# Loading the second layernorm's tiles one by one instead of in pairs

## What is computed

```python
def _layernorm(x, axis=-1, eps=1e-5):
    m = jnp.mean(x, axis=axis, keepdims=True)
    v = jnp.var(x, axis=axis, keepdims=True)
    return (x - m) / jnp.sqrt(v + eps)
...
def _L0_ffn_ref(x, w_gate, w_up, w_down):       # weights int32, scaled by 1/127
    gate = jnp.einsum('bsd,hd->bsh', x, wg)
    up = jnp.einsum('bsd,hd->bsh', x, wu)
    h = jax.nn.silu(gate) * up                   # HIDDEN = 3072
    return jnp.einsum('bsh,dh->bsd', h, wd)
...
x = x + _L0_attn_ref(_layernorm(x, axis=-1), ...)
x = x + _L0_ffn_ref(_layernorm(x, axis=-1), w_gate, w_up, w_down)
```

## Time and profile before

| | us |
|---|---|
| median of 2 runs | 1505.18 (1502.39 to 1507.97) |
| the profiled execution | 1504.06 |
| its span on the slowest core (6) | 1502.5 |
| spans of the other cores | 1481.6 to 1500.1 |
| from the first load of the second layernorm to TensorE's first matmul after it | 824.28 to 993.62 |

### The profile page before, as it was taken

The page is one execution under the profiler, slowest core; times in us unless marked ns, Lnnn a source line. Parts: engine busy times, 40 slices in busy tenths (PEclk is TensorE's granted clock), DMA queues, the critical chain, the costliest instruction groups (busy, mean ns, idle before and its releaser), DMA issues.

```text
span 1502.5 us, 17675 instructions; the slowest of 8 cores (1481.6 to 1502.5 us)
## 1 busy us (share of the span) xinstructions
PE 934.5 (62%) x5815; PEld 446.7 (30%) x5892; DVE 513.6 (34%) x928; ACT 330.7 (22%) x691; POOL 136.0 (9%) x193
## 2 busy tenths in 40 slices
PE   0024365666576666666653000059999999999997
PEld 0002232333233223332331000024444444444443
DVE  0022226456645664566474333102112222210110
ACT  0031622532253315331031121011111111100000
POOL 2000000010101010100010000010111111100100
PEclk9967577778877787688766555579999999999999
DMA  9903220221213121311111334963443443303322
GB/s 143 171 1 97 45 54 0 49 58 50 98 30 71 56 98 29 72 56 43 29 51 70 106 84 91 166 89 33 43 43 31 40 43 39 46 30 112 103 93 98
DMA packets 144456, 99.97 MB, mean 67 GB/s; under 512 B 123504, under 2 KB 123504, under 8 KB 144368
## 3 DMA queue, kind: packets, MB, share of 16 engines
q0 software_dynamic: 72816, 81.02, 26.0%
q1 hardware_dynamic: 71552, 17.83, 6.3%
HBM read 93.86 MB, written 16.78 MB: 74 GB/s over the span
## 4 chain that ended last, share of the span: by engine, by line
PE 52%; DVE 20%; DMA 11%; issue 6%; another core or an unknown queue 5%; ACT 4%; DVEq 1%; SPq 1%; POOL 0%; ACTq 0%; POOLq 0%
PE p_d L952 11%; PE p_g L913 11%; PE p_u L926 11%; PE p_fr L339 5%; DVE s_nL L360 3%; DVE s_nL L435 3%; PE p_py L475 3%; DMA s_wd<-wdi 3%; DMA s_x2T<-s_a 3%; DVE s_ht L667 3%; DMA s_x<-x2d 2%; DVE s_y L731 2%; PE p_fr L475 2%; PE p_pp L575 2%
## 5 line engine op out<-in xcount | busy, mean ns | idle before, releaser
L913 PE MATMUL p_g<-s_x2T,s_wgu 128*128 128x512 bf16 x753 | 181.8, 382 | 181.0 <-DMA s_wgu<-wui 180.2
L926 PE MATMUL p_u<-s_x2T,s_wgu 128*128 128x512 bf16 x752 | 180.0, 379 | 0.8
L952 PE MATMUL p_d<-s_wd,s_hff 128*128 128x512 bf16 x753 | 165.1, 379 | 2.0 <-DVE s_hff L932 1.2
L932 DVE SCALAR_TENSOR_TENSOR s_hff<-p_u,s_act 128x512 bf16<-128x512 f32 x96 | 66.4, 692 | 287.1 <-PE p_u L926 262.1
L913 PEld LDWEIGHTS p_g<-s_x2T,s_wgu 128*128 128x128 bf16 x768 | 75.2, 98 | 272.2 <-issue 182.4
L339 PE MATMUL p_fr<-s_xlnT,s_wg 128*128 128x512 bf16 (+1 forms) x312 | 80.9, 422 | 67.0 <-DMA s_xlnT<-s_xln 60.1
L919 ACT ACTIVATE s_act<-p_g 128x512 f32<-128x512 f32 x96 | 57.3, 597 | 270.1 <-PE p_g L913 270.1
L952 PEld LDWEIGHTS p_d<-s_wd,s_hff 128*128 128x128 bf16 x768 | 74.9, 98 | 92.2 <-issue 1.7
L926 PEld LDWEIGHTS p_u<-s_x2T,s_wgu 128*128 128x128 bf16 x768 | 75.1, 98 | 91.0 <-issue 0.5
L575 PE MATMUL p_pp<-s_wo,s_E 128*128 128x512 bf16 x250 | 72.8, 457 | 25.4 <-DVE s_xr L600 23.4
L705 PE MATMUL p_py<-s_V,s_P 64*64 64x64 bf16 x256 | 29.9, 237 | 89.9 <-DVE s_P L641 89.9
(11 more groups left out here) (109 smaller groups left out, 1131.1 us busy)
## 6 DMA issues: line engine op xcount, KB each, us to landing
s_x<-x2d POOLq DMA_DIRECT2D x32, 512.0 KB, 5.0
s_x<-xs POOLq DMA_DIRECT2D x18, 512.0 KB, 7.6
s_xr<-xs POOLq DMA_DIRECT2D x16, 512.0 KB, 3.8
x2d<-s_xr POOLq DMA_DIRECT2D x16, 512.0 KB, 2.9
out<-s_x POOLq DMA_DIRECT2D x16, 512.0 KB, 3.1
s_wd<-wdi POOLq DMA_DIRECT2D x1, 6144.0 KB, 41.6
s_wgu<-wgi POOLq DMA_DIRECT2D x24, 256.0 KB, 4.3
s_wgu<-wui POOLq DMA_DIRECT2D x24, 256.0 KB, 5.3
```

The lines of the kernel that those rows point to most:

```text
L913: addD("t", lambda t, buf=buf, t4=t4, j=j, pb=pb: t.matmul(p_g[pb][:], s_wgu[buf][:, TILE * j:TILE * (j + 1)], s_x2T[:, 2048 * j + 512 * t ...
L926: addD("t", lambda t, buf=buf, t4=t4, j=j, pb=pb: t.matmul(p_u[pb][:], s_wgu[buf][:, 1024 + TILE * j:1024 + TILE * (j + 1)], s_x2T[:, 2048 ...
L932: addD("v", lambda v, hc=hc, t4=t4, pb=pb: v.scalar_tensor_tensor(s_hff[:, 2048 * hc + 512 * t4:2048 * hc + 512 * (t4 + 1)], p_u[pb][:], S ...
L952: addD("t", lambda t, ts=ts, buf=buf, hf=hf, hcc=hcc: t.matmul(p_d[buf][:, 512 * hf:512 * (hf + 1)], s_hff[:, 2048 * hcc + TILE * ts:2048 ...
```

## The change

The grouping of the loads is taken away. Each tile's load is issued on its own, ahead of that tile's other instructions, with the same wait for the a2 of two tiles before; each tile waits for its own load. Since each load closes the count, each load now also waits on GpSimd until the load before it has landed. Number, size and buffers of the loads are the same.

```diff
-        if tt % 2 == 0:
-            for t2 in (tt, tt + 1):
-                dmaD("g", GX, lambda g, t2=t2: g.dma_start(
-                    out=s_x2[:, 1024 * (t2 % 2):1024 * (t2 % 2 + 1)],
-                    in_=x2d.ap()[TILE * t2:TILE * (t2 + 1), :]),
-                    wait=([(VE, a2_done[t2 - 2])] if t2 >= 2 else []))
-            ld_pair = O.close_epoch(GX)
-        ld = ld_pair
+        dmaD("g", GX, lambda g, tt=tt, buf=buf: g.dma_start(
+            out=s_x2[:, 1024 * buf:1024 * (buf + 1)],
+            in_=x2d.ap()[TILE * tt:TILE * (tt + 1), :]),
+            wait=([(VE, a2_done[tt - 2])] if tt >= 2 else []))
+        ld = O.close_epoch(GX)
```

## The result

| | us |
|---|---|
| before, median of 8 runs | 1506.85 |
| changed kernel, median of 9 runs | 1475.86 (eight of them between 1474.1 and 1478.1) |
| ratio | 0.980, interval 0.9786 to 0.9814 |
| the profiled execution, changed kernel | 1475.86 |
| its span on the slowest core (6 again) | 1474.3 |

The gain is 2.0%, just at the bound of what counts as a change here: 1479 was forecast, with 1471 to 1491 as the range.

A forecast was written before the change was run, and what follows sets the result against it. The layernorm was taken as bound by a latency chain with an unhidden load per pair; six gaps shortened by about 4.05 us each plus 1.3 gave 25.6 off 1504.06, 1478.5, by the median 1479 us; range 1471 to 1491.

The forecast's parts named there:

- The bound: Layernorm tiles, 824 to 944 us: a chain of latencies; each pair pays for an unhidden load, 34.3 us of waiting.
- First tile: Start of the layernorm: load 0 no longer waits for load 1, so the first a2 comes 1.3 us sooner.
- The transpose loop: Layernorm tiles: a2, transpose, next a2 is the longest loop and sets the period, 6.54 us for all 13 gaps.
- The cost of a transpose beside a load need not be guessed: Layernorm tiles: today's odd load, issued 0.58 us behind the even tile's transpose, already shows the order all tiles will have.
- Compute loop: Layernorm tiles: with the transpose landed at once, an a2 follows the a2 before by 4.97 us.
- Load loop: Layernorm tiles: loads issued 1.47 us behind an a2 stay hidden, with 2.5 us of cover at the median.
- The tail: Behind tile 13's a2: down weights still take 41.6 us, so the 25.6 us gained pass to the end whole.
- Rival D: Behind tile 13: down weights take longer or GpSimd stands at load 15; half the gain lost, 1492 us; chance 0.05.
- Rival A: Layernorm tiles: transposes slow down under denser loads, gaps up to 7.6 us, time 1493 us; chance 0.11.
- Rival B: Layernorm tiles: load and transpose take turns, every gap 10.6 us, time 1532 us; chance 0.03.
- Rival C: Layernorm tiles: a period as on core 5 on all cores, 5.91 us, gain 33.8, time 1471 us; chance 0.13.

The follow-up runs named there:

- e1: Changed kernel with two buffers for a2, so an a2 waits for the transpose of two tiles before: 1471.6 us, 0.977 of before.
- e5: Changed kernel with three buffers for loaded tiles and the load of tile tt + 2 issued behind the sum of tile tt: 1459.3 us, 0.971 of before.
- e6: Changed kernel with a small 128x64 fill on GpSimd ahead of each load from tile 2 on: 1467.0 us, 0.977 of before.
- e8: Changed kernel with three load buffers, late loads, down weights in 24 parts, first two blocks' gate and up weights loaded inside the layernorm: 1424.7 us, 0.947 of before.
- e2: Changed kernel with each load from tile 2 on issued only after the sum of the tile before it: 1474.4 us, 0.980 of before.
- e4: Changed kernel with a semaphore for each of the two load buffers, so no load waits for the load before it: 1485.0 us, 0.985 of before.

## Why the prediction was right

Core 6, execution against execution. The span fell by 28.2 us: 29.05 in the 13 gaps (109.29 less 80.24) and 1.2 at the first tile, less 0.4 for a later start, 0.4 in the tail and 1.2 behind the first matmul. The forecast was 25.6. The medians moved by 31.3; the 3 us between that and these two executions are not explained.

- **The bound** (a chain of latencies; each pair pays once for a load): right, the wait of the sum went from 34.3 to 1.1 us.
- **First tile**, 1.3 us: 1.2. From the first load's issue to the first a2 8.93 us before, 7.74 after.
- **The transpose loop sets the period**: right in the changed kernel, as e1 shows. Its **size** was the term most off: 6.54 forecast, 80.24 / 13 = 6.17 on core 6, 5.94 over all cores, both under the 6.2 to 7.1 that I had called the forecast. The a2 waited 24.6 us in 11 gaps where I had written 32 in 13. The two gaps at tiles 8 and 9 give 2.5 of the 4.8 us of difference, and that is luck: nothing in my sum made them short. The remaining 11 on core 6 average (80.24 - 4.97 - 5.63) / 11 = 6.33, the other 2.3 us: I had averaged seven gaps of one core, with 7.12 and 7.60 among them. Over all eight cores those gaps of before average 6.14, close to the 6.06 of the changed kernel outside tiles 8 and 9. The eight-core mean was there to be read.
- **"The cost of a transpose beside a load need not be guessed"**: right, and more so than I knew. The offset stayed at 1.47 us in all but a few tiles, and with it the 5.2 us. I took the 5.2 for what a transpose costs beside a load; it is what it costs beside a load issued at that moment. Where the load comes at 1.82 or later it takes 3.0 to 4.0.
- **Compute loop** 4.97: the exact length of twelve gaps in e5. **Load loop**: I gave it 2.5 us of cover; it ran out only at tiles 9 and 10, where the gaps were short (0.8 and 0.3 us of waiting).
- **The tail** (41.6 us of down weights, passed on whole): 42.1 on core 6; from its issue to that of the next weights 42.5 before and 44.0 after, mean of eight cores. Rival D existed with 1.6 us (first matmul 51.4 us behind tile 13 before, 53.0 after), not with half of the gain.
- **Rival A** (denser loads slow the transposes): landings of 4.6 to 5.7, two of 3.0 and 3.2 aside, against 4.8 to 6.5 before; it did not occur. **Rival B** (taking turns): it did not occur. The rule behind both, that all transfers share the 16 DMA engines, is not refuted, but the size of the cost to the transpose is 2.1 us or nearly nothing, by offset.
- **Rival C** (a period like core 5's) is where the measurement leaned: 5.94 over all cores, and on core 6 a gain close to the 30.1 us asked for over 2%. I had given it 0.13; a mean over cores would have given more.

## What to carry to other kernels

Where two engines start a transfer on the same event, look at the distribution of their landing times and not at the median alone: a few short ones among many long ones (3.2 among 5.2 here) can mean that the overlap costs more at one offset than at another, and a start a third of a microsecond later (1.81 for 1.47 in e6) may be nearly free. Then delay one of the two and measure, as e6 and e5 do. A count that stands for two loads makes the first reader wait for the second load; one count for each was worth 4.4 us for each pair here (28.5 us over the 13 gaps, mean of eight cores), most of a load's 5.1. And what follows the repaired chain is the next bound: here one transfer of 42 us that nobody needed for over 300 us, in front of 6 us of weights that everybody waited for.

## What the runs showed of the hardware

- A DMA transpose of a 128x1024 bf16 tile took 4.1 to 6.5 us when the next 512 KB load from GpSimd was issued 1.4 to 1.7 us behind the start of the a2 (all of 462 transposes of tiles 0 to 12, in all kernels here but e8), and 3.0 to 4.0 us when it was issued at 1.82 or later (all of 461). From 1.70 to 1.82 both occur, 61 of 197 over 4 us, and there the cores differ: 51 of 97 took over 4 us on cores 0, 2, 4 and 6, 10 of 100 on cores 1, 3, 5 and 7. Why is open.
- The packets in the trace (the pieces in which the DMA engines move a transfer) say what is slow. A transpose is 1,024 packets of 256 bytes and 32 of 4 bytes. In the changed kernel 87 transposes took over 4 us and 17 less. The last 256-byte packet of the 87 ended 3.5 to 3.6 us behind the start of the a2, just as that of the 17 (3.5 to 3.8). The last 4-byte packet ended at 3.5 to 3.8 in the 17 and at 4.7 to 6.4 in the 87. So the overlap does not slow the data, it holds up the small packets that close the transfer, and the next a2 waits for those. Where the load was issued before the transpose or together with it (the first tile of e5) it was otherwise: there the 256-byte packets themselves ended at 4.9 to 5.6.
- What holds the small packets is not shown. That the load's instruction (0.53 us) ends before the transpose's own (0.9 + 1.23 = 2.1) does, as it does at 1.47, is not the condition: at 1.65 to 1.81 it ends behind it, at 2.2 to 2.3, and transposes of over 4 us still occur. That a small packet can stand behind those of another transfer agrees with the Trainium skill, page "DMA: Bandwidth & Descriptors", section "Queues, rings and completion order", by which a DMA engine changes between its queues packet by packet; the page gives no cost for it, here it is 2.1 us.
- The load pays too, but little by little: median landing 4.9 us in the changed kernel, 3.6 in e2 with its loads at 2.8 or later. From 1.47 to 1.81 it hardly changed (4.2 to 5.9 us with the fill ahead of it on core 2 of e6, 4.6 to 5.6 on core 6 of the changed kernel).
- Beside the down weights, a transfer of 39 to 45 us in the two kernels, the transpose of tile 14 took 16 to 20 us instead of 3 and that of tile 15 12 to 19 (19.3 and 16.9 on core 6 of the changed kernel).
- In the changed kernel the load of tile 9 was issued 0.29 us later than its neighbours, at the offset 1.76, on all eight cores, and the gap behind it was 4.97 to 4.99 us. In e4 the same happened to the load of tile 10. Nothing in the program differs there. What delays GpSimd at this instruction is open.
